# Moving x and out two batches per transfer in a conditioned residual kernel

## The reference, cut to what matters

```python
x       : (64, 128, 2048) float32     # B batches, C channels, T time
itok    : (64,) int32, 0 <= itok < 16 # one state per batch
weights : (16, 128, 128) float32      # S states, C channels, D features

W = weights[itok]
out = x + einsum('bct,bcd->bdt', x, W)
```

## Time and profile before

| | |
|---|---|
| Median of 3 runs | 327.18 us (326.92 to 327.31) |
| Span of the profiled execution | 324.3 us |
| Moved by DMA | 135.27 MB, mean 417 GB/s over the span |
| TensorE matmul busy | 231.8 us (71%) |
| VectorE busy | 146.7 us (45%) |
| GpSimd busy | 19.0 us (6%) |
| Chain that ended last | 90% waits for loads of x |
| Load of x, issue to landing | 19.6 us median, 1024 KB |
| Store of out, issue to landing | 19.5 us median, 1024 KB |

### The profile page before, as it was taken

One profiled execution on the slowest core, in us unless ns is written; L12 is line 12 of the kernel. 1 busy time (PEld: TensorE's weight loads), 2 busy tenths in 40 slices (PEclk: granted clock), 3 DMA queues, 4 the chain that ended last, 5 costly groups with the idle time before them and its releaser, 6 DMA issues.

```text
span 324.3 us, 2750 instructions
## 1 busy us (share of the span) xinstructions
PE 231.8 (71%) x512; PEld 94.7 (29%) x512; DVE 146.7 (45%) x64; ACT 0.2 (0%) x1; POOL 19.0 (6%) x69
## 2 busy tenths in 40 slices
PE   0039999999999867867768768678677687686200
PEld 0014444444444322322322323223223223232000
DVE  0005576676676554453553543534535535435200
ACT  0000000000000000000000000000000000000000
POOL 0010010010000000000000000000000000000000
PEclk9999999999999999999999999999999999999755
DMA  7999999999999999999999999999999999999995
GB/s 282 384 412 420 427 428 426 427 428 426 425 427 427 427 428 426 427 425 429 425 427 428 426 429 425 427 426 429 424 427 428 426 428 427 426 425 428 427 426 234
DMA packets 18962, 135.27 MB, mean 417 GB/s; under 512 B 2066, under 2 KB 2066, under 8 KB 2578
## 3 DMA queue, kind: packets, MB, share of 16 engines
q10 hardware_dynamic: 9746, 68.16, 49.9%
q1 hardware_dynamic: 9216, 67.11, 49.5%
HBM read 68.16 MB, written 67.11 MB: 417 GB/s over the span
## 4 chain that ended last, share of the span: by engine, by line
DMA 90%; PE 1%; SPq 1%; DVE 1%; issue 1%; DVEq 0%
DMA x_ring<-x 90%; PE product L105 1%; SPq L63 1%; DVE x_ring L127 1%; DVEq L127 0%
## 5 line engine op out<-in xcount | busy, mean ns | idle before, releaser
L105 PE MATMUL product<-x_ring,chosen_weights 128*128 (+1 forms) x512 | 231.8, 603 | 70.2 <-POOL chosen_weights L85 66.4
L127 DVE TENSOR_TENSOR x_ring<-product,x_ring 128x2048 f32 x64 | 146.7, 2292 | 157.8 <-PE product L105 157.8
L105 PEld LDWEIGHTS product<-x_ring,chosen_weights 128*128 128x128 f32 x512 | 94.7, 191 | 206.5 <-issue 206.4
L85 POOL COPY chosen_weights<-weight_table 128x128 f32 x64 | 18.8, 293 | 264.0 <-PE product L105 236.0
L140 ACT MOVE_SHAPE weight_table<-weights x1 | 0.2, 160 | 1.4 <-PEq L157 1.4
L157 POOL MEMSET const-float32-0.0<- 128x1 f32 x1 | 0.1, 98 | 0.1
L157 POOL MEMSET const-bfloat16-1.0<- 128x1 bf16 x1 | 0.1, 101 | 0.0
L157 POOL MEMSET const-uint8-127<- 128x1 uint8 x1 | 0.1, 101 | 0.0
L157 POOL MEMSET const-float32-1.0<- 128x1 f32 x1 | 0.1, 98 | 0.0
L157 POOL BASE_LOAD x1 | 0.0, 17 | 0.2 <-issue 0.2
## 6 DMA issues: line engine op xcount, KB each, us to landing
x_ring<-x SPq DMA_DIRECT2D x64, 1024.0 KB, 19.6
out<-x_ring ACTq DMA_DIRECT2D x64, 1024.0 KB, 19.5
condition_row<-condition ACTq DMA_DIRECT2D x1, 0.2 KB
weight_table<-weights ACTq DMA_DIRECT2D x1, 0.5 KB, 18.2
```

The costliest lines, as they stand in the source:

```text
L85: pool.tensor_copy(chosen_weights[u][:, :], weight_table[:, bass.ds(state * features, features)]).then_inc(weights_chosen, 1)
L105: last = pe.matmul(product[:, u % psum_slots, m * BANK_COLUMNS:(m + 1) * BANK_COLUMNS], chosen_weights[u][:, :], x_ring[:, bass.ds(ring_co ...
L127: dve.tensor_tensor(tile, product[:, u % psum_slots, :], tile, AluOpType.add).then_inc(sum_done, 1)
```

## The change

A transfer of x or out now covers two batches, 2 MB: per channel two rows of 8 KB, which lie 1 MB apart in memory and side by side in the ring. The ring has 8 slots of 16 KB per partition, the same bytes. There are 8 turns of 4 steps. Four loads and four stores are still in flight at most, each of twice the size. POOL, PE and DVE still work batch by batch; there are 8 copies `chosen_weights` instead of 4; PE waits for a load at every second batch, and a store waits for the second sum of its pair. The table and the states are loaded as before.

```diff
--- before.py
+++ after.py
@@ -16,15 +16,17 @@
 
 BANK_COLUMNS = 512
 PSUM_BANKS = 8
+BATCHES = 2
 STEPS = 4
-RING_TURNS = 4
+RING_TURNS = 2
 
 
 def conditioned_residual(nc, x, condition, weights, out):
     fp32 = mybir.dt.float32
     batches, channels, time = x.shape
     states, _, features = weights.shape
-    turns = batches // STEPS
+    turns = batches // (STEPS * BATCHES)
+    group = BATCHES * time
     matmuls = time // BANK_COLUMNS
     psum_slots = PSUM_BANKS // matmuls
 
...
-        x_ring = sbuf("x_ring", [channels, RING_TURNS * STEPS * time])
+        x_ring = sbuf("x_ring", [channels, RING_TURNS * STEPS * group])
         weight_table = sbuf("weight_table", [channels, states * features])
-        chosen_weights = [sbuf(f"chosen_weights{u}", [channels, features]) for u in range(STEPS)]
+        chosen_weights = [sbuf(f"chosen_weights{b}", [channels, features]) for b in range(STEPS * BATCHES)]
...
         def ring_column(turn, u):
 
-            return (turn % RING_TURNS) * (STEPS * time) + u * time
+            return (turn % RING_TURNS) * (STEPS * group) + u * group
+
+        def batches_of(tensor, turn, u):
+            first = turn * (STEPS * BATCHES) + u * BATCHES
+            return tensor[bass.ds(first, BATCHES)].rearrange("b c t -> c b t")
+
+        def ring_group(turn, u):
+            return x_ring[:, bass.ds(ring_column(turn, u), group)].rearrange("c (b t) -> c b t", b=BATCHES)
 
         block = ctx.enter_context(nc.Block())
 
         @block.sync
         def _(sp):
             def load(turn, u):
-                sp.dma_start(x_ring[:, bass.ds(ring_column(turn, u), time)],
-                             x[bass.ds(turn * STEPS + u, 1)].rearrange("b c t -> c (b t)")
-                             ).then_inc(x_loaded[u], 16)
+                sp.dma_start(ring_group(turn, u), batches_of(x, turn, u)).then_inc(x_loaded[u], 16)
 
...
-            def choose(turn, u):
-                state = pool.value_load(condition_row[0:1, bass.ds(turn * STEPS + u, 1)],
+            def choose(turn, b):
+                state = pool.value_load(condition_row[0:1, bass.ds(turn * (STEPS * BATCHES) + b, 1)],
                                         min_val=0, max_val=states - 1)
-                pool.tensor_copy(chosen_weights[u][:, :],
+                pool.tensor_copy(chosen_weights[b][:, :],
                                  weight_table[:, bass.ds(state * features, features)]
                                  ).then_inc(weights_chosen, 1)
 
             pool.wait_ge(condition_loaded, 16)
             pool.wait_ge(table_loaded, 16)
-            for u in range(STEPS):
-                choose(0, u)
+            for b in range(STEPS * BATCHES):
+                choose(0, b)
             with pool.Fori(1, turns) as turn:
-                for u in range(STEPS):
+                for b in range(STEPS * BATCHES):
 
-                    pool.wait_ge(product_done, (turn - 1) * STEPS + u + 1)
-                    choose(turn, u)
+                    pool.wait_ge(product_done, (turn - 1) * (STEPS * BATCHES) + b + 1)
+                    choose(turn, b)
 
...
-            def multiply(turn, u):
-                pe.wait_ge(x_loaded[u], 16 * (turn + 1))
-                pe.wait_ge(weights_chosen, turn * STEPS + u + 1)
+            def multiply(turn, b):
+                u, within = divmod(b, BATCHES)
+                if within == 0:
+                    pe.wait_ge(x_loaded[u], 16 * (turn + 1))
+                pe.wait_ge(weights_chosen, turn * (STEPS * BATCHES) + b + 1)
                 for m in range(matmuls):
-                    last = pe.matmul(product[:, u % psum_slots, m * BANK_COLUMNS:(m + 1) * BANK_COLUMNS],
-                                     chosen_weights[u][:, :],
-                                     x_ring[:, bass.ds(ring_column(turn, u) + m * BANK_COLUMNS, BANK_COLUMNS)],
+                    last = pe.matmul(product[:, b % psum_slots, m * BANK_COLUMNS:(m + 1) * BANK_COLUMNS],
+                                     chosen_weights[b][:, :],
+                                     x_ring[:, bass.ds(ring_column(turn, u) + within * time + m * BANK_COLUMNS,
+                                                       BANK_COLUMNS)],
                                      start=True, stop=True)
                 last.then_inc(product_done, 1)
 
...
-                for u in range(STEPS):
-                    pe.wait_ge(sum_done, turn * STEPS + u - psum_slots + 1)
-                    multiply(turn, u)
+                for b in range(STEPS * BATCHES):
+                    pe.wait_ge(sum_done, turn * (STEPS * BATCHES) + b - psum_slots + 1)
+                    multiply(turn, b)
 
...
-                for u in range(STEPS):
-                    tile = x_ring[:, bass.ds(ring_column(turn, u), time)]
+                for b in range(STEPS * BATCHES):
+                    u, within = divmod(b, BATCHES)
+                    tile = x_ring[:, bass.ds(ring_column(turn, u) + within * time, time)]
 
-                    dve.wait_ge(product_done, turn * STEPS + u + 1)
-                    dve.tensor_tensor(tile, product[:, u % psum_slots, :], tile,
+                    dve.wait_ge(product_done, turn * (STEPS * BATCHES) + b + 1)
+                    dve.tensor_tensor(tile, product[:, b % psum_slots, :], tile,
                                       AluOpType.add).then_inc(sum_done, 1)
 
...
-                act.wait_ge(sum_done, turn * STEPS + u + 1)
-                act.dma_start(out[bass.ds(turn * STEPS + u, 1)].rearrange("b c t -> c (b t)"),
-                              x_ring[:, bass.ds(ring_column(turn, u), time)]
-                              ).then_inc(out_stored[u], 16)
+                act.wait_ge(sum_done, turn * (STEPS * BATCHES) + (u + 1) * BATCHES)
+                act.dma_start(batches_of(out, turn, u), ring_group(turn, u)).then_inc(out_stored[u], 16)
 
...```

On SP the first part of the program issues the loads of the first turns. These are the rows of before at its start:

```order
L60 UNCONDITIONAL_BRANCH [waits barrier_Pool_Activation_PE_DVE_SP_release]
L63 DMA x_ring<-x 128x2048 x4
L70 UNCONDITIONAL_BRANCH
L70 ISA
L63 ISA [waits x_loaded0]
L63 DMA x_ring<-x 128x2048
```

6 lines of the change are left out of this document (3 added, 3 removed).

## The result

The changed kernel takes 324.88 us (median of 4 runs, 324.5 to 325.16) beside 327.09 us before (4 runs). The ratio is 0.994, with a 95% interval of 0.9926 to 0.9955: 2.2 us faster. Repeated in later rounds (`after_again`) it was 0.9946 (0.9934 to 0.9959). In what follows every ratio and every time leaves out executions that were over 1.5% slower than the fastest of the same kernel; only the profiles of `halves`, `tiny_loads` and `more_instructions` are of such slower executions.

What follows compares the result with a forecast made beforehand. The prediction took the bytes through full DMA engines as the bound. It summed -0.6 us (semaphore packets) and +0.3 (first load) to -0.3, all else zero: span 324.0, time 326.9 us, range 325.2 to 328.5.

Steps and rivals of the forecast that it cites:

- The bound: Whole span: full DMA engines, 135.27 MB at 427 GB/s taking 316.8 us of 324.3 us.
- Semaphore packets: End of each transfer: 64 fewer 4-byte packets on each engine, taken as -0.6 us.
- the first load: Start: x's three-dimensional access issues later, +0.5 us at most, up to +1.0 with doubled packet generation; taken as +0.3.
- The 0.56 us that a larger first transfer might fill: From 2 to 4 us: engines only 72% full, so a larger first transfer might gain 0.56 us.
- The table: Start: the load all computation waits for might land 0 to about 4 us later, hidden by the ring; zero.
- the first store: Start: it needs two sums and comes 3.4 us later, covered by loads going on alone; zero.
- the ring: Middle: SP will wait for stores; loads take about 24 us, stores 39, and the queues never empty; zero.
- the end: After the last load, near 294 us, 27 us of stores hide the last pair's 9.4 us; the tail stays.
- The trailing engine: Tail: one DMA engine's 2.9 us lag, unchanged if lost by bytes, -1.5 us if by transfer; taken as 0.
- The rival at 325.4 us: Tail: the trailing engine pays at each transfer, so its 2.9 us halve; faster, chance 0.20.
- The base: Time outside the span: the median of the runs taken as 2.9 us above the 324.3 us span, left unchanged.
- The adverse rivals: Slower: rows 1 MB apart, 329.8 us (0.08); longer start, 328.2 (0.08); DMA idle behind a late table, 337 (0.04).

Runs made afterwards that it cites:

- halves: The kernel before with each load and each store split into two of 64 channels: 363.15 us, ratio 1.1108.
- tiny_loads: The changed kernel with four extra loads of 16 rows of 8 bytes behind each 2 MB load, 128 in all: 333.6 us, ratio 1.0208.
- more_instructions: The kernel before with six needless reads of a state per batch on GpSimd: one run at 328.16 us, five from 344.96 to 357.1.
- load1_store4: The changed kernel with loads of 1 MB, four in flight, and stores of 4 MB, two in flight: 328.71 us, ratio 1.0062.
- body8: The kernel before with its 1 MB transfers, only the loops changed to 8 turns of 8 batches: 325.97 us, ratio 0.9978.
- load1_store2: The changed kernel with loads of 1 MB instead of 2 MB, stores still 2 MB: 325.45 us, ratio 0.9954.
- load2_store1: The changed kernel with stores of 1 MB instead of 2 MB, loads still 2 MB: 326.35 us, ratio 0.9982.
- big2_flight2: The kernel before with 2 MB transfers in loops of 8 turns, only two loads and two stores in flight: 324.99 us, ratio 0.9945.
- four_mb: The changed kernel with loads and stores of 4 MB, two of each in flight: 331.41 us, ratio 1.0145.
- store_cols: The kernel before with every store issued as two transfers of 1024 columns, in 4 KB packets: 334.4 us, ratio 1.023.

## Why the prediction was wrong

**The bound** was right: the bytes, at a full share in both kernels. The first add starts at 28.39 us (26.69 before) and the last load packet ends at 290.7 (forecast near 294).

**Semaphore packets and the first load.** The small packets fell by 1024, but their -0.6 us can't be seen: most engines are done at 320.5 and 320.4 us, and 32 fewer loads alone, which take away 512 of them, leave the ratio at 0.9982 beside 0.9978. The first load's +0.3 had no such cause: SP's four loads are issued in the same time as before, with no MOVE_SHAPE ahead. The timelines from 0 to 6 us, before and after:

```profile
0.80 2.04 SPq L63 DMA_DIRECT2D x_ring<-x  x4
...
0.80 2.05 SPq L72 DMA_DIRECT2D x_ring<-x  x4
```

The 0.56 us that a larger first transfer might fill didn't come either. From 2 to 4 us the share rises from 0.72 to 0.97, and the rate doesn't rise with it (283 GB/s before):

```profile
2.00:4.00 2.00, 0.00 (x0) 0.00 (x0) 0.00 (x0) 0.00 (x0) 0.00 (x0) 1.00 0.97 279
```

What the start did lose is 375 after 377 GB/s over 34 us, 0.2 us.

**The table, the first store, the ring, the end.** Right in that all stay hidden; SP now waits for stores. Its waits in the changed kernel:

```profile
SPq L84 <- DMA out<-x_ring: 166.0, 18, 9.9
SPq L72 <- DMA out<-x_ring: 60.3, 6, 16.4
```

That is 24 waits where there was none, and the share stays at 1.01. Stores at 38.6 us were right (39); loads land after 16.3 us, not 24. At half of 428 GB/s these are an estimated 3.5 MB of loads outstanding, near the lower end of the 3.2 to 5.3 MB that I counted.

**The trailing engine** is the step that failed. I had sized both answers, 0 by bytes and -1.5 us by transfer, and took 0, "as it carries every byte and the halving needs a cost that only one engine in sixteen has". The runs show a loss that goes with how the stores are cut: the same loads, waits and bytes give 0.9981 with 1 MB stores and 0.994 with 2 MB stores, 1.1 to 1.3 us where I had put 0. The rival at 325.4 us, to which I gave 0.20, comes near the case, though not as told: only the stores matter, and a fixed loss for each is not shown, as 19 stores do no better than 32. That its -1.5 us are near the measured term is partly luck, since it counted the loads too.

**The range** left out the prediction's own low end. The bounds of the sum gave 324.5 to 328.2, which holds 324.88, but the range was stated from 325.2. The chances don't add up as told either: by their parts they are 0.28 faster, 0.50 same and 0.22 slower.

**The base.** 2.9 us around the span was the median of some runs less the span of a shorter one; within one run it is 2.0 us. Against the median span of 325.0 the trailing engine's lag in the kernel before was about 0.7 us longer than in the tail that I read, and so was what the change could take from it. The profile could not show that; the range should have held it.

**The adverse rivals** did not come: two rows 1 MB apart run at 428 GB/s. The argument against them was weaker than told, though: loads alone do not run at the full rate in the rows (403 and 410 GB/s in the earlier trace rows). The warning of the Trainium skill, "DMA: Bandwidth & Descriptors", section "Latency and other measured facts", is of the pitch from one partition's row to the next, which stays at 8 KB, so no run here shows a case of it. The Trainium skill has in "DMA: Bandwidth & Descriptors", section "Measured (HBM→SBUF, 128 partitions, SWDGE, issued from GpSimd)", a rate that rises with the size of a transfer. Here the sign holds for stores and the size does not: 0.4% from 1 to 2 MB, in the tail, none from 2 to 4 MB, and none for loads.

What stays open is why one engine trails at all, why the stores' cut moves it, and the 0.4 to 0.7 us by which every kernel of the table with 1 MB stores, the unchanged one loaded anew included, came out below its comparison.

## What to carry to other kernels

When all DMA engines are full, look at the last microseconds column by column: this kernel ends with its slowest engine, and that was worth more than anything in the middle. Profile twice before a forecast of under 1%, state a range that holds the bounds of your own sum, and compare spans with the median span of the runs, not one span with the median time. Larger groups pay only while the transfers left over cover the computation of the last group; split that last group if they don't.

## What the runs showed of the hardware

- One of the 16 DMA engines falls behind while all are full, by 0.18 and 0.22 us in a turn of 8.39 MB in the two profiles of the kernel before, and ends 2.4 to 3.4 us after the others. Where the engines idle before the end (`load1_store4`), all stop together.
- Transfers over 64 channels in place of 128, with the same packets of 8 KB, move 376 GB/s at a full share, and the kernel takes 363 us in place of 327.
- With rows of 4 KB in place of 8 KB, in the stores or in the loads, a full share moves 417 GB/s in place of 427; the kernels take 2.3% and 2.9% longer, the second partly from an idle stretch at its end.
- 128 stores of 16 rows of 8 bytes between full ones cost about 0.13 us each.
- The granted clock of TensorE goes with the size of the loads: 0.97 to 0.99 on the mean in runs with four loads of 1 MB in flight (`body8`, `load1_store2`, `load1_store4`), 0.92 to 0.94 with loads of 2 MB (`load2_store1`, `big2_flight2`, the changed kernel), 0.90 with 4 MB (`four_mb`). `store_cols` is an exception, 0.92 to 0.94 with loads of 1 MB. Before, PE rests 1.2 to 1.3 us after each batch between 110 and 140 us; in the changed kernel it works through two batches and then rests 1.0 to 2.7 us. Its matmuls took 240.3 us in place of 231.8, and the DMA share stayed at 1.01. That the rests are the cause was not tested.
- With six more reads for each batch on GpSimd the adds came every 4.9 us on the mean from 122 to 294 us, the pace at which the DMA engines move a batch in and out (2.10 MB at 427 GB/s), and every 5.1 to 5.6 us from 307 us on. The slower pace showed only after the last load packet, at 297.4 us, when nothing but stores was left and each waits for its sum: the share falls from 1.01 to 0.69 between 290 and 310 us.
